# Mixture-of-experts block on one core: a signal and a wait between consecutive result scatters

## What is computed

```python
logits = x @ gate_w.T
topv, topi = jax.lax.top_k(logits, TOP_K)                 # TOP_K = 8 of 64 experts
rw = jax.nn.softmax(topv.astype(jnp.float32), axis=-1).astype(x.dtype)
W = jnp.zeros((N, E), x.dtype).at[jnp.arange(N)[:, None], topi].set(rw)
gu = jnp.einsum('nh,eih->nei', x, gu_w)
gate, up = (gu[..., :I], gu[..., I:])
inter = jax.nn.silu(gate) * up
inter_w = inter * W[:, :, None]
out = jnp.einsum('nei,ehi->nh', inter_w, dp_w)
...
out = out + sh_g * sh_out
```

## Time and profile before

| what | us |
|---|---|
| median of 3 runs | 1209.91 |
| lowest and highest of them | 1209.32, 1215.4 |
| span of the profiled execution, from the first to the last instruction | 1382.2 |
| PE busy in that span | 1080.5 |
| POOL busy in that span | 722.5 |
| first to last scatter of results, by start | 821.0 to 1359.0 |

### The profile page before, as it was taken

The page is one execution under the profiler, slowest core; times in us unless marked ns, Lnnn a source line. Parts: engine busy times, 40 slices in busy tenths (PEclk is TensorE's granted clock), DMA queues, the critical chain, the costliest instruction groups (busy, mean ns, idle before and its releaser), DMA issues.

```text
span 1382.2 us, 23533 instructions
## 1 busy us (share of the span) xinstructions
PE 1080.5 (78%) x7305; PEld 833.1 (60%) x7305; DVE 703.8 (51%) x2197; ACT 647.6 (47%) x1586; POOL 722.5 (52%) x953
## 2 busy tenths in 40 slices
PE   3799998888888888889765058887888878787875
PEld 1566666565565656566534047777777767676763
DVE  3476766666666666656525411121245544444447
ACT  2465656555555555655331024444445444444441
POOL 3111225657466564564566735655565565655552
PEclk9699999999999989989877569999999999998996
DMA  2586877212122121122228855555767777776536
GB/s 82 174 288 221 275 256 237 101 48 95 51 84 93 53 90 51 59 102 61 84 93 289 269 172 161 172 169 154 238 233 251 268 268 248 259 243 238 170 138 212
DMA packets 142824, 233.18 MB, mean 169 GB/s; under 512 B 17303, under 2 KB 119910, under 8 KB 137840
## 3 DMA queue, kind: packets, MB, share of 16 engines
q1 hardware_dynamic: 67936, 101.06, 22.7%
q0 software_dynamic: 27600, 69.28, 14.1%
q10 hardware_dynamic: 47168, 61.35, 13.5%
HBM read 107.32 MB, written 132.53 MB: 174 GB/s over the span
## 4 chain that ended last, share of the span: by engine, by line
PE 46%; DVE 16%; another core or an unknown queue 14%; issue 13%; ACT 8%; POOL 1%; DMA 1%; ACTq 0%; SPq 0%; DVEq 0%; POOLq 0%
PE psB L1412 6%; DVE nmax L868 6%; PE psD L1429 5%; PE psv L607 4%; PE ps L511 4%; PE psA L1402 4%; PE ps L558 3%; PE ps L518 3%; PE psp L490 3%; PE psp L504 3%; PE psC L1420 3%; ACT xT L1297 2%; ACT y L1313 2%; PE psq L634 2%
## 5 line engine op out<-in xcount | busy, mean ns | idle before, releaser
L1497 POOL DMA_INDIRECT res_d<-y,dst_i x319 | 320.9, 1006 | 231.9 <-ACT y L1313 117.8
L463 POOL DMA_INDIRECT rows_d<-pay,slot_i x256 | 256.5, 1002 | 75.4 <-issue 73.4
L868 DVE TENSOR_REDUCE nmax<-ps 128x1 f32<-128x512 f32 (+3 forms) x448 | 225.8, 531 | 135.8 <-PE ps L518 93.5
L736 ACT ACTIVATE wgu_s<-ps 128x512 f32<-128x512 f32 x320 | 191.9, 600 | 123.4 <-PE ps L518 91.3
L1216 DVE TENSOR_TENSOR inner<-inner,psB 128x128 f32<-128x128 f32 x160 | 45.8, 286 | 316.8 <-ACT inner L1302 250.5
L1429 PE MATMUL psD<-wdp_s,innerT 128*128 x638 | 174.8, 397 | 21.1 <-ACT innerT L1306 17.6
L1412 PE MATMUL psB<-wgu_s,xT 128*128 x1276 | 179.1, 285 | 1.2 <-ACT xT L1297 0.8
L518 PE MATMUL ps<-mask,ident_b 128*128 128x256 bf16 (+1 forms) x640 | 175.4, 274 | 0.4 <-issue 0.4
L511 PE MATMUL ps<-kT,qT 96*128 96x512 f32 (+3 forms) x512 | 168.3, 391 | 8.1 <-DVE nmax L868 4.8
L558 PE MATMUL ps<-qT,kT 128*128 128x512 f32 (+3 forms) x512 | 165.8, 387 | 4.9 <-ACT wgu_s L736 4.2
L1412 PEld LDWEIGHTS psB<-wgu_s,xT 128*128 128x128 f32 x1276 | 163.9, 201 | 1.8 <-issue 1.2
(11 more groups left out here) (256 smaller groups left out, 1620.0 us busy)
## 6 DMA issues: line engine op xcount, KB each, us to landing
rows_d<-blank ACTq DMA_DIRECT2D x8, 5440.0 KB, 19.3
xg<-rows_d SPq DMA_DIRECT2D x160, 272.0 KB
yk<-res_d SPq DMA_DIRECT2D x28, 1024.0 KB
wgu_s<-wgu_in ACTq DMA_DIRECT2D x8, 1024.0 KB
x_d<-x SPq DMA_DIRECT2D x30, 192.5 KB
xs<-x_d SPq DMA_DIRECT2D x30, 192.5 KB, 2.5
res_d<-y,dst_i POOLq DMA_INDIRECT x319
wgu_s<-x_in SPq DMA_DIRECT2D x32, 128.0 KB, 2.2
```

The lines of the kernel that those rows point to most:

```text
L463: pool.indirect_dma_start(rows_d, bass.IndirectOffsetOnAxis(ap=slot_i[par][:, t, k:k + 1], axis=0), pay[par][:, t, :], None).then_inc(s_sc ...
L736: act.activation(pexp[p % 4][:, s, :], ps2[:, (5 * p + s) % 2, :], ACT.Exp, scale=HEAD_D ** -0.5).then_inc(s_exp, 1)
L868: return dve.tensor_reduce(nmax[u][:, tile, heads[0]:heads[-1] + 1], src, AX.X, ALU.max, negate=True)
L1497: pool.indirect_dma_start(res_d, bass.IndirectOffsetOnAxis(ap=dst_i[:, j % (2 * G):j % (2 * G) + 1], axis=0), y[:, j % Y, :], None, bounds ...
```

## The change

A semaphore `e_sent` (`scatter_issued`) is added. Each result scatter now carries it as the engine's own completion signal: the Pool adds 1 to it when it has finished the instruction, that is, written the descriptors and started the transfer. That is not the landing, which `e_out` still tells. Ahead of every scatter but the first one the Pool waits until `e_sent` has counted all scatters before it. The wait is an instruction of its own on the Pool and stands after the waits for `e_dst` and `e_d`, ahead of the register move and of the indirect DMA. Nothing changes its place, on the Pool or on any other engine: there are 319 scatters before and after, and 318 waits are added.

```diff
@@ -1015,6 +1015,7 @@
             e_front, e_back = sem("pe_step_front"), sem("pe_step_back")
+            e_sent = sem("scatter_issued")
 
             e_x = [sem(f"xg_in{k}") for k in range(G // 2)]
@@ -1494,9 +1495,11 @@
                     if j % 2 == 0:
                         pool.wait_ge(e_d, j // 2 + 1)
+                    if j > 0:
+                        pool.wait_ge(e_sent, j)
                     pool.indirect_dma_start(
                         res_d, bass.IndirectOffsetOnAxis(ap=dst_i[:, j % (2 * G):j % (2 * G) + 1], axis=0), y[:, j % Y, :], None,
-                        bounds_check=ROUTED - 1, oob_is_err=False).then_inc(e_out[j % Y], 16)
+                        bounds_check=ROUTED - 1, oob_is_err=False, engine_sem=e_sent).then_inc(e_out[j % Y], 16)
```

## The result

| | before | after |
|---|---|---|
| median, us | 1211.37 (1209.32 to 1215.4, 4 runs) | 1372.7 (1368.62 to 1373.23, 4 runs) |
| ratio to before | | 1.1334, 95% interval 1.1315 to 1.1354 |
| span of the profiled execution, us | 1382.2 | 1370.7 |

The change makes the kernel slower by 161 us, 13%. The two profiles alone would say the opposite: the span of after is 11 us shorter. The reason is that the profiled execution of before was an unusual one. The twelve executions profiled behind it, one of the kernel before among them, have spans within 0.5% of the median of their kernel. Against this second profile, 117.5 us of what the first execution took longer lie between the first and the last scatter and 54.7 us ahead of them.

A forecast was written before the change was run, and what follows sets the result against it. The prediction took PE and unexplained stalls to bound the experts before, the Pool after: 318 x 1.85 = 587 us, less 447 us, costs 140 us. So 1210 + 140 = 1350 us, range 1250 to 1410.

The forecast's parts named there:

- The gap: Pool idle time between consecutive result scatters after the change: 0.84 us, bounds 0.45 and 1.0, making a step 1.85 us.
- The three rows that carried it: Profile rows with an idle Pool and an indirect DMA: scatter starts 0.78 to 0.85 us after its release.
- The present length of the experts: Expert stage of the kernel before without a profile: 447 us, the middle of two estimates, 423 and 471 us.
- the Pool's own floor: Shortest time in which the Pool could do its 318 scatter steps before the change: 417 us, 1.31 us each.
- The share-out by unexplained waits: Splitting the profile's extra 172 us by unexplained waits: 115 us falls to the experts, leaving 423 us.
- an even share: Spreading the profile's extra 172 us evenly over the execution: 538 x 1210/1382 = 471 us for the experts.
- the missing 172 us: Excess of the profiled execution before over the median, said to come from stalls, not Pool or PE work.
- What bounds the kernel: Experts before the change: bound by PE and unexplained stalls, the Pool having about 121 us to spare.
- What would show it: Profile after: gaps about 0.84 us without bursts, scatters 575 to 600 us, PE busy 70 to 75%, copy waits grown.
- Rival 1: Dispatch is still prepared while the Pool waits: 1.46 us a step, 1210 to 1227 us, likeliest 1212; chance 0.09.
- Rivals 2 and 3: Freer DMA queues shrink PE and ACT stalls, 1200 us, chance 0.03; completion signal later than recorded end, about 1490, chance 0.07.
- Rival 4: PE, waiting for the Pool, falls to the lower clock and slows: perhaps 10 us, inside the range; no chance given.

The follow-up runs named there:

- experiment 9: The kernel before, unchanged, profiled a second time: span 1207.6 us, 420.5 us from first to last scatter, time 1209.41 us.
- experiments 5 to 7: Against the kernel before: one Pool memset added ahead of each scatter, 1266.71 us; two, 1347.02 us; second gate and up product left out on PE, 1206.81 us.
- experiment 3: The changed kernel with the wait attached to the indirect DMA itself, behind the register move: 1213.71 us, ratio 1.0028.
- experiment 2: The changed kernel with each scatter waiting for the one before the last: 1213.01 us, ratio 1.0020.
- experiment 10: The changed kernel with the index bound put into its register once, ahead of the loop: 1286.82 us, ratio 1.0629.
- experiments 1 and 3: Against the changed kernel: signal kept but no wait, 1210.64 us; wait attached to the indirect DMA itself, 1213.71 us.
- experiment 11: The kernel before with scatters without an index bound, padded rows going to spare rows in `res_d`: 1204.82 us, ratio 0.9942.
- experiment 7: The kernel before with the second gate and up product of each block left out on PE: 1206.81 us, ratio 0.9975.

## Why the prediction was right

The time (1350 us forecast, 1372.7 measured), the sign and the mechanism of the gap were right. What was wrong is the picture of the kernel before: it was already bound by the Pool. Point by point:

- **The gap.** 0.84 us was taken, between the bounds 0.45 and 1.0. Measured 0.84 in the mean. The step was to be 1.85 us and is 1.835 (583.4 / 318); the stretch was to be 587 us and is 583.4. The three rows that carried it were of the right kind: in the trace the waits behind the earlier trace rows stand in a wait instruction or on the register move, ahead of their DMA, as the new one does. Of the bounds, the 0.15 us for a semaphore and the 0.15 us for a late signal stand in no row; the signal comes 0.01 us after the recorded end.
- **The present length of the experts.** This term was mis-sized: 447 us was taken, and it is 420.5. With 420.5 the sum would have been 587 - 420.5 = 166.5 and 1376 us, 4 us over what was measured, which is the step's 1.85 for 1.835. The 417 us taken as the lower end, the Pool's own floor, was almost exact. The share-out by unexplained waits gave 423 us (115 us of the 172 in the experts; it was 117.5) and was close too; taking the middle between it and an even share, for which no reason was given, made the forecast some 26 us too low. The premise under all of it was wrong as well: I took the missing 172 us for something that every profile adds, and experiment 9 shows that a profile adds nothing here. That this did the sum no harm is luck: whether a profile adds stalls or one execution was unusual, the runs have shorter experts than the profile showed. Nor was it so that PE's work couldn't give a part of the 172 us: PE is busy for 1080.5 us in the first profile and for 1024.8 in the second, with a higher granted clock.
- **What bounds the kernel.** "The experts are bound by PE and by those unexplained stalls" was true of the execution that was read and false of the kernel. In an undisturbed one the Pool is the bound already before the change (experiments 5 to 7), so next to no part of the new wait could be hidden.
- **What would show it.** No bursts, right. The releaser is the scatter before, right for 265 of the waits. The waits of the copy to y grew, right: 290.1 us. PE busy for 70 to 75% of the experts: it is 76 to 80% in the stretches shown and 78% (457 of 583 us) over all scatters. Its work took longer than the 401 us of the second profile of before, where its granted clock was 0.99 in place of 0.91. The span near the median: right, 1370.7 and 1372.7, but not for the reason that was given, since the undisturbed profile of before shows the same.
- **Rival 1**, the cheap wait, did not come about for this edit, but its mechanism exists: experiment 3 is that case, with a gap of 0.30 us where 0.45 was reckoned. What I held against it, "the trace doesn't agree for waits that stand in an instruction of their own", was right in substance, but half of the new waits are carried by a register move instead; what counts is that they are not on the DMA. The 0.15 us that I added for the semaphore isn't there.
- **Rivals 2 and 3.** No gain appears anywhere, and the signal is not late: in experiment 3 the whole way from the end of a scatter over its signal to the start of the next one takes 0.30 us.
- **Rival 4.** The granted clock did fall, from 0.99 over the stage to about 0.90, and PE is busy for 56 us more over the scatters. None of it is seen in the time: 318 steps of the Pool's own 0.99 + 0.84 us are the whole stretch.

## What to carry to other kernels

In this kernel an indirect DMA on the Pool starts 0.76 to 0.87 us after a release if its preparation has to wait for that too, and 0.30 us after the one before it if the Pool's instruction stream may run ahead: half a microsecond a piece. A wait on something recent should therefore sit on the DMA itself, with register moves and long-met waits ahead of it (experiment 3), or look one DMA further back (experiment 2). Which instruction ends up with a wait is read from the trace, not from the source: in experiment 10 half of the waits landed elsewhere. And before a slack read from one profile is believed, its span has to be compared with the runs: here 118 us of slack in the experts belonged to one unusual execution, and the Pool, busy for 76% of the stage while PE was busy for 96%, was the bound all along, through the 0.30 us behind each of its scatters.

## What the runs showed of the hardware that was not expected

- An indirect DMA that waits for the completion of the one before it starts 0.30 us after that one's end, exactly as without a wait (experiment 3: 0.30 us; experiment 9: 0.30 us). The signal comes 0.01 us after the recorded end (experiments 1 and 3), and it fits with the release into a gap that is there anyway.
- With the wait on a register move or in an instruction ahead of it, the next instruction of the stream starts 0.03 us after the end of the scatter before, and the scatter 0.74 us after its register move (the changed kernel).
- A scatter with a bound on its indices takes the Pool 985 ns in the median, one without it 963 ns, although the latter writes the padded rows as well that the former skips (experiment 11, which also has no register move).
- PE can be recorded busy for 401 of 420 us (96%) and still not be the bound: 51 us less of it shortened the run by 3 us (experiment 7).
